# A recommendation tower on one core: where the first table's ids are compared, who compares the last table's, and the place of one transpose

## The reference

```python
e = jnp.stack([tbl_0[ids[:, 0]], tbl_1[ids[:, 1]], ..., tbl_25[ids[:, 25]]], axis=1)
all_emb = jnp.concatenate([r_bottom_output[:, None, :], e], axis=1)      # 512 x 27 x 128
gram = jnp.einsum('bfd,bgd->bfg', all_emb, all_emb)
z = gram[:, _TRIU_I, _TRIU_J]                                            # 512 x 351
h = jnp.concatenate([z, r_bottom_output], axis=1)
h = jnp.maximum(h @ W_top1 + b_top1, 0.0)                                # 479 -> 512
h = jnp.maximum(h @ W_top2 + b_top2, 0.0)                                # 512 -> 256
y = h @ W_top3                                                           # 256 -> 1
```

## Time and profile before

| | us |
|---|---|
| median of 3 runs | 112.02 (111.33 to 112.22) |
| the profiled execution | 113.11 |
| its span in the profile | 111.3 |
| PE busy | 102.7 (92%) |
| DVE busy | 67.5 (61%) |
| ACT busy | 62.0 (56%) |
| POOL busy | 55.9 (50%) |

### The profile page before, as it was taken

How to read it: one execution, slowest core, us unless ns; L and a number is a source line. 1 busy time by engine, 2 the same in 40 slices (tenths; PEclk the granted TensorE clock), 3 DMA queues, 4 the chain that set the end, 5 groups by cost and what they waited for, 6 DMA issues and landing times.

```text
span 111.3 us, 3670 instructions
## 1 busy us (share of the span) xinstructions
PE 102.7 (92%) x1562; PEld 87.2 (78%) x1562; DVE 67.5 (61%) x151; ACT 62.0 (56%) x105; POOL 55.9 (50%) x59
## 2 busy tenths in 40 slices
PE   4999999999999999899958999976999989999992
PEld 4767778887888887788947889865999978997970
DVE  3599999999999989999980006400910550082010
ACT  5535996992894899986573124242343246234331
POOL 2777787777777777777777777740000000000000
PEclk9999999999999999999999999999999999999999
DMA  2989999999999999999961212220000000000000
GB/s 73 286 243 233 198 236 211 235 228 221 204 223 236 208 229 231 229 198 226 239 175 47 53 53 53 68 56 0 6 6 0 6 6 0 6 9 0 0 0 0
DMA packets 6369, 13.72 MB, mean 123 GB/s; under 512 B 1984, under 2 KB 2640, under 8 KB 6354
## 3 DMA queue, kind: packets, MB, share of 16 engines
q1 hardware_dynamic: 4520, 10.02, 39.6%
q0 software_dynamic: 1664, 3.41, 13.5%
q10 hardware_dynamic: 170, 0.07, 0.3%
HBM read 13.48 MB, written 0.02 MB: 121 GB/s over the span
## 4 chain that ended last, share of the span: by engine, by line
PE 49%; POOL 24%; issue 12%; DMA 9%; ACT 3%; ACTq 0%
POOL rows L328 24%; PE acc L683 11%; PE acc L649 10%; DMA rows<-tbl,ids_sb 7%; PE ring L693 7%; PE acc L614 6%; PE acc L588 6%; PE acc L674 3%; PE ring L626 3%; PE ring L703 2%; DMA ids_sb<-ids 2%; PE ring L657 1%; ACT emb L400 1%; ACT onehot L389 1%; ACT away L384 0%
## 5 line engine op out<-in xcount | busy, mean ns | idle before, releaser
L328 POOL DMA_INDIRECT rows<-tbl,ids_sb x52 | 55.2, 1061 | 17.2 <-issue 15.5
L498 DVE TENSOR_SCALAR onehot<-far 125x512 fp32r<-125x512 f32 x102 | 38.2, 434 | 1.9 <-ACT far L359 1.9
L588 PE MATMUL acc<-onehot,hi 125*128 125x512 f32 x94 | 26.2, 404 | 0.2 <-DVE onehot L498 0.2
L588 PE MATMUL acc<-onehot,lo 125*128 125x512 f32 x94 | 25.0, 390 | 0.0
L508 DVE COPY gram<-acc 128x432 f32<-128x432 f32 x4 | 3.7, 922 | 29.8 <-PE acc L649 29.8
L588 PEld LDWEIGHTS acc<-onehot,lo 125*128 125x128 f32 x94 | 17.7, 188 | 3.8
L588 PEld LDWEIGHTS acc<-onehot,hi 125*128 125x128 f32 x94 | 16.7, 188 | 4.8 <-DVE onehot L498 1.7
L345 ACT CAST hi<-raw 125x1024 fp32r<-125x1024 f32 (+1 forms) x12 | 13.3, 1105 | 11.3 <-DMA raw<-tbl 6.8
L485 DVE TENSOR_TENSOR lo<-raw,hi 125x512 fp32r<-125x512 f32 (+1 forms) x26 | 18.4, 710 | 0.0
L649 PE MATMUL acc<-emb 128*27 128x27 f32 x1024 | 12.9, 192 | 2.7 <-issue 2.7
L649 PEld LDWEIGHTS acc<-emb 128*27 128x27 f32 x1024 | 10.9, 104 | 5.1 <-issue 3.5
(11 more groups left out here) (41 smaller groups left out, 77.9 us busy)
## 6 DMA issues: line engine op xcount, KB each, us to landing
raw<-tbl SPq DMA_DIRECT2D x9, 448.0 KB
raw<-tbl SPq DMA_DIRECT2D x3, 560.0 KB
ids_b<-ids SPq DMA_DIRECT2D x4, 256.0 KB, 10.6
rows<-tbl,ids_sb POOLq DMA_INDIRECT x52, 8.3
w1z<-w SPq DMA_DIRECT2D x1, 702.0 KB
w_sb<-w SPq DMA_DIRECT2D x1, 512.0 KB
raw<-tbl SPq DMA_DIRECT2D x9, 52.0 KB
raw<-tbl SPq DMA_DIRECT2D x2, 224.0 KB
```

The costliest lines, as they stand in the source:

```text
L328: nc.gpsimd.indirect_dma_start(out=rows[:, t, slot, :], out_offset=None, in_=tables[table], in_offset=bass.IndirectOffsetOnAxis(ap=ids_sb[ ...
L498: ins = nc.vector.tensor_scalar(onehot[:, n % OH_RING, k, :], far[:, t % FAR_RING, :], float(c), None, ALU.is_equal)
L588: mm = nc.tensor.matmul(acc[:, look_bank(t), :], part_of[:, t % HL_RING, c * D:(c + 1) * D], onehot[:, n % OH_RING, k, :], start=(half == ...
```

## The change

Three edits. (1) For table 0 the one-hot chunks are no longer compared from `far` but straight from the PSUM bank of the spread ids, with the row number of the chunk (`row_f`, 125x8, per-partition scalar) in place of the constant; ACT makes no `far` for that table. `row_f` takes one more iota on POOL and one small copy on DVE. (2) Table 12 is no longer `by_act`: DVE makes all eight of its chunks. (3) The turn (3, 3) stands ahead of the bottom step (2, 1), no longer behind it.

```diff
-              ("gram", 2, 2), ..., ("turn", 3, 2), ("bottom", 2, 1),
-              ("turn", 3, 3),
+              ("gram", 2, 2), ..., ("turn", 3, 2), ("turn", 3, 3),
+              ("bottom", 2, 1),
...
 def by_act(j):
-    return LOOKED_UP[j] in LONG or paired(j)
+    return LOOKED_UP[j] in LONG or paired(j) and j < NL - 1
...
+        row_n = sb("row_n", [KP, KCS[0]], I32)
+        row_f = sb("row_f", [KP, KCS[0]])
+        row_first = sem("row_first")
...
         def _(pool):
+            nc.gpsimd.iota(row_n[:], pattern=[[1, KCS[0]]], base=0, channel_multiplier=KCS[0]).then_inc(row_set, 1)
...
                     if t == 0:
-                        difference(0)
                         act.wait_ge(idt_ready, 1)
...
-                        act.wait_ge(far_ready, t + 1)
+                        act.wait_ge(far_ready, t)
...
-            dve.wait_ge(row_set, len(KCS))
+            dve.wait_ge(row_set, len(KCS) + 1)
             nc.vector.tensor_scalar(neg_row[:], row_i[:], -1.0, None, ALU.mult).then_inc(row_ready, 1)
+            nc.vector.tensor_copy(row_f[:], row_n[:]).then_inc(row_first, 1)
...
                 if step == "compare":
-                    dve.wait_ge(far_ready, t + 1)
+                    if t == 0:
+                        dve.wait_ge(ids_spread, 1)
+                        dve.wait_ge(row_first, 1)
+                    else:
+                        dve.wait_ge(far_ready, t)
...
-                            ins = nc.vector.tensor_scalar(onehot[:, n % OH_RING, k, :], far[:, t % FAR_RING, :], float(c),
-                                                          None, ALU.is_equal)
+                            if t == 0:
+                                ins = nc.vector.tensor_scalar(onehot[:, n % OH_RING, k, :], acc[0:KP, spread_bank(0), :],
+                                                              row_f[:, c:c + 1], None, ALU.is_equal)
+                            else:
+                                ins = nc.vector.tensor_scalar(onehot[:, n % OH_RING, k, :], far[:, t % FAR_RING, :],
+                                                              float(c), None, ALU.is_equal)
```

More of the change, by code:

```diff
@@ L114, in work_order @@
               ("gram", 2, 0), ("l2", 0, 0), ("gram", 2, 1), ("l2", 0, 1), ("pairs", 1, 0), ("bottom", 2, 0),
-              ("gram", 2, 2), ("l1", 1, 0), ("l1", 1, 1), ("gram", 2, 3), ("l1", 1, 2), ("l1", 1, 3), ("turn", 3, 2), ("bottom", 2, 1),
-              ("turn", 3, 3),
+              ("gram", 2, 2), ("l1", 1, 0), ("l1", 1, 1), ("gram", 2, 3), ("l1", 1, 2), ("l1", 1, 3), ("turn", 3, 2), ("turn", 3, 3),
+              ("bottom", 2, 1),
               ("gram", 3, 0), ("l2", 1, 0), ("gram", 3, 1), ("pairs", 2, 0), ("l2", 1, 1), ("l3", 0, 0),
```

## The result

The changed kernel takes 112.94 us in the median of 20 runs (112.39 to 114.67), the kernel before 112.19 in the median of 20 of its own (111.33 to 114.06). The ratio is 1.007, with a 95% interval of 1.0047 to 1.0093: 0.75 us slower, within 1%. A ratio compares the undisturbed runs of two kernels and a median takes in all of them, so the two can differ. The prediction was 112.9, with 0.64 for within 1%, and a loss of 0.91.

The account below looks back on a forecast made before the run. A chain of DVE's comparisons was taken to bound the kernel up to about 60 us, then PE. S - 0.33 + 0.36 - 0.86 gave +0.91 us on the 112.02 median: 112.9, range 111.5 to 113.8.

Parts of the forecast that it names:

- The start: DVE begins table 0's compares at 4.03 us instead of 4.75, after the first spread matmul: 0.72 us earlier.
- The price: Table 0's eight compares from PSUM pace at 0.67 us each, against 0.36 from SBUF.
- the case of no overlap: Table 0's PSUM compares pace at 0.70 to 0.75 us: +1.15 to +1.55 us, 113.2 to 113.6; 22%.
- the one at SBUF's pace: Table 0's PSUM compares keep 0.36 to 0.43 us, leaving only a 0.50 us gain: 111.5; 9%.
- the outlier at 0.93: Table 0's compares pace at 0.93 us, like a PSUM copy: +2.99 us, 115.0; 2%.
- The absorption: PE's turn at 27.48 us and the waits up to table 9 take up 0.33 us, leaving S - 0.33.
- S: How much later DVE comes to table 1, after table 0's PSUM compares: +1.74 us.
- S - 0.83: Whole change: S - 0.33 arriving, + 0.36 for one more DVE compare, - 0.86 slack at the last table: +0.91 us.
- 0.50: Last table: dropping ACT's chunk opens 0.86 us of slack, DVE's extra compare spends 0.36; alone a 0.50 us gain.
- The clock: PE, idle early on, falls to the lower clock for one half look, 1.8 us later: +2.7 us, 114.7; 6%.
- The tail: In the second stretch, what PE gains or loses by 60 us reaches the end one for one.
- the vanishing of its stalls: 2.1 us of PE's unexplained waits in gram fall away: -1.2 us, 110.8; 6%.

Follow-up runs that it names:

- e4_sbuf_scalar: Changed kernel, but table 0 compared from far in SBUF again, with the chunk number as per-partition scalar; 169.98 us, loads arriving late.
- e3: Changed kernel with table 1 compared from PSUM too, run twice with late loads: 166.44 us beside 161.83, and 165.87 beside 162.28 for the kernel before.
- changed_again: The changed kernel unaltered, profiled a second time, with late loads: 162.79 us beside 162.28 for the kernel before, ratio 1.002.
- e1_psum_again: Kernel before with only table 0's compares from PSUM, second run, loads arriving late: ratio 1.0113 to the kernel before.
- e2_last_again: Kernel before with only table 12's eight chunks all by DVE, second run: 111.86 us beside 112.94, ratio 0.998.
- e6_last_bot: Kernel before with table 12 all by DVE and ACT's copy of the bottom vector moved ahead of table 12's cast: 112.00 us beside 112.94, ratio 0.9941.

## Why the prediction was right

**The start** was right: DVE begins at 3.97, predicted 4.03, released by PE's spread matmul as foreseen.

**The price** was right in its sum and less so in its parts. The compare from PSUM lasts 745 ns; 533 + 218 = 751 had been worked out from a one-element step and the fixed part of the one `tensor_scalar` from PSUM in the earlier trace rows. It does overlap with the next, so it paces at 0.66 (predicted 0.67), and the case of no overlap falls, as do the one at SBUF's pace and the outlier at 0.93. The Trainium skill's 120 + 512 cycles, 0.66 us ("VectorE: DVE Perf Modes", errata table), agrees with the trace's pace. The part for the per-partition scalar, 0.04 to 0.06 from SBUF by e4_sbuf_scalar, was missing. If it costs as much from PSUM, the source alone was overrated by as much, some 0.3 us over eight compares, and that 0.67 came out was luck; if it costs nothing there, the price was right. No run tells which.

**The absorption** was right step by step. S is 1.60 (predicted 1.74); 0.33 less arrives at the turn, at ACT's run and at table 9 (1.27, 1.27, 1.28), and DVE's wait shrinks to 0.29 (predicted about 0.3; 0.56 less 0.33 would be 0.23).

**Edit 2** inside the changed kernel worked the way it was foreseen: no wait for ACT, one more compare, DVE's `lo` the gate. The formula S - 0.83, which follows DVE's chain, held: with the measured S it gives 0.77; the last half start shows 0.68, the medians 0.75. As a split between the edits it did not: edit 1 alone came to 0.85 at the last half and not S - 0.33 = 1.27, since ACT's chain was then the gate, and edit 2 gave 0.18 on top, not 0.50. Alone, its 0.50 was neither confirmed nor refuted by time; its trace shows 0.20, behind a wait at table 9 that had grown.

**Edit 3** is nothing, as predicted. In the changed kernel the two copies and gram (3, 0) read as in the earlier trace rows:

```profile
89.51 0.88 ACT L423 COPY emb<-ring 128x512 f32<-128x512 f32 x2
...
90.49 0.73 PE L662 MATMUL acc<-emb 128*27 128x27 f32 x64 [0.54 <-issue]
```

The wait is 0.54 us in both, and the copies are back to back and take 0.88 in both. It was not tried alone, but the right column of the table bounds it: 30.25 us in both profiles of the changed kernel, 30.28 or 30.29 in the three of edit 1 alone, and 30.30 to 30.63 in e3 and e4, which have edit 3 too. So it gains 0.03 at most, which is what the prediction allowed.

**The clock** did not fall in the changed kernel's first profile. PE stood idle for 1.11 us before 9.99, and its four matmuls then took 1.21 us, as fast as before. In changed_again, the same program, the first half look ran at the lower pace, behind the same idle time of 0.69 us:

```profile
6.78 2.08 PE L601 MATMUL acc<-onehot,hi 125*128 125x512 f32 x4 [0.69 <-DVE onehot L508]
```

So what the change does to PE's idle time there doesn't decide it. Nor did it cost the rival's 1.8 us: PE, which has idle time to give at this place, was at the turn at 19.75 and not 19.64.

**The tail** was taken to pass the shift on one for one, with the vanishing of its stalls as the rival for a faster kernel. One for one is what the medians show. The rival named the right place but not its nature: the stalls vary by execution.

## What to carry to other kernels

An operation that reads its operand many times wants it in SBUF: one pass of 0.69 us on an otherwise free engine pays for eight compares that would each be 0.26 us dearer from PSUM, and an earlier start (0.78 us here) is soon eaten. A shift of one engine should be followed from wait to wait through the kernel, since waits for something that doesn't move (gathered rows) give part of it back, and two edits that meet at the same gate need not add up: where two chains meet, a delay may reach one with 1.27 us and the other with 0.85. And where a kernel's tail varies by half a microsecond from one execution to the next, compare the stages that were touched in the profiles, and the whole only in medians.

## What was not expected of the hardware

- The pace of PE's first half look differs between executions, of one and the same program too: four matmuls in 1.18 to 1.21 us in eight profiles, in 2.02 to 2.08 in the other six (changed_again, e1_psum_again, e2_last_again, both of e3, e6_last_bot), with the same work of PE ahead of it, while the granted clock reads 1.00 from 1 to 12 us in all. The spread matmuls run at about that lower pace in all profiles (1.92 to 2.05 us for four). (2.02 - 0.63) / 3 = 0.46 us a matmul, with 0.63 for a single spread matmul, is twice the 0.227 of later ones, as the levels of 1.2 and 2.4 GHz are apart.
- A per-partition scalar instead of a constant makes a 125x512 compare from SBUF last 481 ns instead of 423 to 434 (the means of all profiles), 0.04 to 0.06 us more in pace.
- The same kernel can take 162 us instead of 112 in one run after another, with DVE and ACT idle in the middle for tens of microseconds, behind loads as I read it, while its compares and its tail read as ever.
